# Three-layer graph network: FP32 rows and FP32 adjacency blocks in place of split BF16 ones, and 14 dense tiles in layer 1 in place of 10

## The reference, cut to what matters

```python
# x: 6250 x 256 FP32 nodes, 100000 edges sorted by dst, and a self loop on each node
deg  = segment_sum(1, dst);  dinv = rsqrt(deg);  norm_edge = dinv[src] * dinv[dst]
h = x
for W, b in ((W1, b1), (W2, b2), (W3, b3)):     # 256->512, 512->512, 512->256
    m = h @ W
    h = relu(segment_sum(m[src] * norm_edge[:, None], dst) + b)
out = layernorm(x + h)
```

## Time and profile before

| what | before |
|---|---|
| median of three runs (2494.5 to 2496.02) | 2496.0 us |
| the profiled execution's own time | 2488.2 us |
| its span, first to last instruction | 2486.4 us |
| PE busy / PEld busy | 2271.8 us (91%) / 1562.8 us (63%) |
| POOL busy | 1753.4 us (71%) |
| DVE / ACT busy | 1027.0 us (41%) / 521.7 us (21%) |
| mean granted clock of TensorE | 0.965 of full speed |
| moved by DMA | 568.24 MB, 229 GB/s |

### The profile page before, as it was taken

How to read it: one execution, slowest core, us unless ns; L and a number is a source line. 1 busy time by engine, 2 the same in 40 slices (tenths; PEclk the granted TensorE clock), 3 DMA queues, 4 the chain that set the end, 5 groups by cost and what they waited for, 6 DMA issues and landing times.

```text
span 2486.4 us, 42327 instructions
## 1 busy us (share of the span) xinstructions
PE 2271.8 (91%) x13351; PEld 1562.8 (63%) x13352; DVE 1027.0 (41%) x1307; ACT 521.7 (21%) x1322; POOL 1753.4 (71%) x1837
## 2 busy tenths in 40 slices
PE   6977799898999998999999999999988799999998
PEld 6855577676777773444444444444444688888887
DVE  8877333233333313444444444444422233333332
ACT  6611223222222312222222222222211000000000
POOL 5177777777777756777777777777776776767674
PEclk9788999999999999999999999999999899999999
DMA  6335666666666656888888888888887888888784
GB/s 215 119 118 184 222 203 206 201 198 205 192 209 190 208 170 204 253 272 268 267 264 264 263 267 264 264 268 258 275 260 236 261 257 249 252 248 255 245 247 140
DMA packets 231550, 568.24 MB, mean 229 GB/s; under 512 B 39868, under 2 KB 95795, under 8 KB 231475
## 3 DMA queue, kind: packets, MB, share of 16 engines
q0 software_dynamic: 126752, 399.62, 54.6%
q1 hardware_dynamic: 88371, 126.81, 14.5%
q10 hardware_dynamic: 16352, 40.77, 4.9%
HBM read 476.69 MB, written 90.36 MB: 228 GB/s over the span
## 4 chain that ended last, share of the span: by engine, by line
PE 55%; POOL 16%; issue 13%; DMA 7%; POOLq 4%; DVE 3%; ACT 0%; ACTq 0%; DVEq 0%; SPq 0%
POOL rows L671 16%; PE ps_acc L1511 9%; PE ps_h L1600 8%; PE ps_T L1600 7%; PE ps_o L1567 6%; DMA rows<-table,idx 5%; PE ps_d L1612 5%; PE ps_acc L1515 5%; PE ps_d L1515 4%; PE ps_h L1555 3%; PE ps_d L1511 3%; POOLq L680 3%; PE ps_d L1469 2%; DMA rows<-table_parts,idx 1%; PE ps_e L1588 1%
## 5 line engine op out<-in xcount | busy, mean ns | idle before, releaser
L671 POOL DMA_INDIRECT rows<-table,idx x912 | 870.0, 954 | 300.9 <-issue 264.7
L671 POOL DMA_INDIRECT rows<-table_parts,idx x884 | 837.1, 947 | 324.0 <-issue 268.2
L892 DVE SCALAR_TENSOR_TENSOR sel<-ps_e,firsts,dstT 128x1152 f32<-128x1152 f32 (+1 forms) x222 | 314.7, 1418 | 684.9 <-PE ps_acc L1511 253.9
L1515 PE MATMUL ps_acc<-rows,sel 128*128 128x512 f32 (+2 forms) x1122 | 489.8, 568 | 82.8 <-DMA rows<-table,idx 55.5
L1515 PE MATMUL ps_d<-rows,sel 128*128 128x512 f32 (+1 forms) x850 | 413.3, 616 | 41.3 <-DMA rows<-table,idx 41.2
L1511 PE MATMUL ps_acc<-rows,sel 128*128 128x256 bf16 (+1 forms) x2196 | 360.1, 280 | 50.5 <-DMA rows<-table_parts,idx 21.7
L1515 PEld LDWEIGHTS ps_acc<-rows,sel 128*128 128x128 f32 x1122 | 209.2, 202 | 250.0 <-issue 149.3
L1511 PEld LDWEIGHTS ps_acc<-rows,sel 128*128 128x128 bf16 x2196 | 217.9, 100 | 93.9 <-issue 37.8
L1515 PEld LDWEIGHTS ps_d<-rows,sel 128*128 128x128 f32 x850 | 152.8, 195 | 196.4 <-issue 119.2
L1567 PE MATMUL ps_o<-w,hT 128*128 128x512 f32 (+1 forms) x784 | 269.2, 486 | 1.2 <-ACT hT L1272 1.2
L1612 PE MATMUL ps_d<-parts,made_tiles 128*128 128x256 bf16 x1470 | 229.2, 272 | 0.5 <-issue 0.4
(11 more groups left out here) (190 smaller groups left out, 1902.8 us busy)
## 6 DMA issues: line engine op xcount, KB each, us to landing
built<-made_tiles SPq DMA_DIRECT2D x72, 384.0 KB
made_tiles<-built ACTq DMA_DIRECT2D x72, 384.0 KB
rows<-table,idx POOLq DMA_INDIRECT x912
rows<-table_parts,idx POOLq DMA_INDIRECT x884
table<-made SPq DMA_DIRECT2D x49, 256.0 KB
acc<-table SPq DMA_DIRECT2D x49, 256.0 KB
built<-made_tiles SPq DMA_DIRECT2D x24, 416.0 KB
made_tiles<-built ACTq DMA_DIRECT2D x24, 416.0 KB
```

The source lines that it names most:

```text
L671: pool.indirect_dma_start(out=to, out_offset=None, in_=its[0:nodes, :], in_offset=bass.IndirectOffsetOnAxis(ap=idx[:, of, k:k + 1], axis=0 ...
L892: v.scalar_tensor_tensor(to[:, k:k + FRONT, :], numbers.unsqueeze(1).broadcast_to([P, FRONT, P]), firsts[:, bass.ds(t, 1)], dstT[:, bass.d ...
L1515: return mm(to[:, 0:w], sel[:, k, :], rows_of[phase][:, k, 0:w] if first is None else first, start=start, stop=stop)
```

## The change

The BF16 parts are gone from all of it: `parts`, `table_parts`, `split_x`, `split`, the stores of parts and the waits for them. `whole` (128 x 49 x 256 FP32) takes the place of `parts`; layer 1 holds x scaled there, and layer 2's ACT writes its result straight into it, without waiting for `made_free`. Every gathered slot of layers 1 and 3 is one FP32 product of 256 columns.

A dense step is one FP32 product too, and its block must be FP32: a single buffer `wide` (128 x 49 x 128). ACT fills it from the BF16 block, piece by piece (`widen`, four copies of 1664 or 1536 columns for a tile), each as soon as PE has used that piece of the dense tile before (`dense_piece`). PE waits for each piece (`widened`). In layer 3, ACT loads the block after next once a piece is widened.

In layer 1, 14 tiles are dense and 35 gathered: seven plain windows, then 14 macros of two windows each. The loop of two macros runs six times. Layer 2 builds 10 blocks in place of 14, in its first 30 windows.

```diff
-DENSE_1 = 10
+DENSE_1 = 14
-PARTS = 3
-    PER = 3
+    PER = 2
-        parts = sb("parts", [P, T, PARTS, C], BF16)
-        xs = parts[:, :, :, :].rearrange("p t i c -> p (t i c)")[:, 0:2 * T * C].bitcast(F32).rearrange(
-            "p (t c) -> p t c", c=C)
+        whole = sb("whole", [P, T, C])
+        xs = whole
+        wide = sb("wide", [P, T, P])
...
-                        if phase == 2:
-                            pool.wait_ge(parts_stored, 16 * (T - 1))
...
-            def split_x(units):
...
-            def split(t):
...
+            def widen(q, of, pieces):
+
+                for piece in pieces:
+                    lo_h, hi_h = PIECES[piece]
+                    act.wait_ge(dense_piece, len(PIECES) * q + piece + 1)
+                    act.sem_inc(act_step, 1)
+                    nc.scalar.activation(wide[:, lo_h:hi_h, :], making[of][:, lo_h:hi_h, :], ACT.Copy).then_inc(widened, 1)
+
+            def widen_built(m, of, pieces):
+                act.wait_ge(self_added, m + 1)
+                widen(m, of, pieces)
...
@@ ACT, first window of a macro
                             scale_dense(m - 1)
+                            widen(m, 1 - of, range(len(PIECES) - 1, len(PIECES)))
+                            if half is not None:
+                                keep_pairs(*half, range(0, PAIRS // 2))
                             keep_aggT(s, aggT[:, 0:C], 0)
+                            if half is not None:
+                                keep_pairs(*half, range(PAIRS // 2, PAIRS))
                             relus(s)
...
+                    if build:
+                        widen_built(m + 1, of, range(len(PIECES) - 1))
...
-                if in_parts:
-                    row = rows_parts[:, k, :] if first is None else first
-                    for i in range(PARTS):
-                        ins = mm(to[:, 0:C], sel_parts[:, k, :], row[:, i * C:(i + 1) * C], start=start and i == 0,
-                                 stop=stop and i == PARTS - 1)
-                    return ins
...
-                    for i in range(PARTS):
-                        ins = mm(ps_dense_1, making[of][:, h, :], parts[:, h, i, :], start=(h == 0 and i == 0),
-                                 stop=(h == T - 1 and i == PARTS - 1))
+                    wait_widened(k, h)
+                    ins = mm(ps_dense_1, wide[:, h, :], whole[:, h, :], start=(h == 0), stop=(h == T - 1))
...
-                DENSE_CUTS = [0, 11, 29, T]
+                DENSE_CUTS = [0, 16, T]
```

More of the change, by code:

```diff
@@ L389, in gnn_program @@
         y_d_stored = sem("y_d_stored")
-        X_UNITS = [(47 - 2 * i, 2, False) for i in range(22)] + [(3, 2, True), (1, 2, True), (0, 1, True)]
-        X_DONE = [0, 0, 2, 5, 9, 15, 21, len(X_UNITS)]
-        assert T == 49 and ASIDE == 5 and len(X_DONE) <= MACRO
+        assert MACRO > 6
         block = ctx.enter_context(nc.Block())
@@ L492, in store @@
                         w = WIDTH[phase + 1]
-                        sp.dma_start(table[phase + 1][bass.ds(t * P, P), :], made[:, 0:w]).then_inc(stored, 16)
+                        its = made[:, 0:w]
+                        if phase == 1 and per == 1:
+                            its = whole[:, bass.ds(t, 1), :].rearrange("p a c -> p (a c)")
+                        sp.dma_start(table[phase + 1][bass.ds(t * P, P), :], its).then_inc(stored, 16)
                         sp.wait_ge(stored, 16 * s + 16)
@@ L1111, in macro @@
                         steady(0, MACRO + PER * m + b, (MACRO + PER * odd + b) % 2, hots,
-                               (m, place_of(m, True), of) if b == 0 else None, last=not build and b == PER - 1, in_parts=True)
+                               (m, place_of(m, True), of) if b == 0 else None, last=not build and b == PER - 1)
                 macro(0, 0, 0)
@@ L1119, in one_window, with six @@
                 to_next(0)
-                def six(i, first=False):
+                def six(i):
                     for b in range(6):
@@ L1128, in six @@
                                (q, place_of(q, False), u) if part == 2 else None)
-                        if not first or b > 0:
-                            split(t - 2)
-                six(0, True)
-                with v_.Fori(1, SIXES) as i:
+                with v_.Fori(0, SIXES) as i:
                     six(i)
@@ L1282, in relus, with make @@
                     relu_T(ps_h[:, m * P:(m + 1) * P], b1T, m)
[L1284 removed]
+            def make(phase, t, s, per=1):
                 w = WIDTH[phase + 1]
                 act.wait_ge(o_done, s + 1)
[L1287 removed]
+                if phase == 1 and per == 1:
+                    to = whole[:, bass.ds(t, 1), :].rearrange("p a c -> p (a c)")
+                else:
+                    to = made[:, 0:w]
+                    act.wait_ge(made_free, s + 1)
                 act.sem_inc(act_step, 1)
[L1289 removed]
+                nc.scalar.activation(to, ps_o[:, 0:w], ACT.Copy, scale=dinv[:, bass.ds(t, 1)]).then_inc(made_ready, 1)
             def tile(phase, t, n, s, per, built_half=None):
@@ L1516, in add_slot, with slots @@
                           start=start, stop=stop)
-            def slots(phase, n, ks, first, need=None, beside=None, ps=None, in_parts=False):
+            def slots(phase, n, ks, first, need=None, beside=None, ps=None):
                 to = ps_acc if ps is None else ps
@@ L1590, in build, with wait_widened @@
                 ins.then_inc(pair_built, 1)
+            def wait_widened(q, h):
+                for piece, (lo_h, _) in enumerate(PIECES):
+                    if h == lo_h:
+                        pe.wait_ge(widened, len(PIECES) * q + piece + 1)
             def dense(i, into, hs):
```

260 lines of the change are left out of this document (86 added, 174 removed).

## The result

| | before | after |
|---|---|---|
| median of the runs | 2495.25 us (four runs, 2490.92 to 2496.02) | 2799.02 us (four runs, 2796.4 to 2802.53) |
| profiled execution, span | 2488.2 us, 2486.4 us | 2799.73 us, 2798.0 us |

The changed kernel is slower: the ratio is 1.1222, with a 95% interval of 1.1203 to 1.1242. The forecast was 2800 us, and slower with a chance of 0.97.

What follows compares the result with a forecast made beforehand. PE was taken to bound layers 1 and 3, POOL layer 2. 147.2 - 5.4 + 163.2 = +305.0 on the profiled 2488.2 us gives 2793.2; for a median 2801, rounded to 2800 us, range 2765 to 2840.

Steps and rivals of the forecast that it cites:

- Prices: On PE, a step or slot goes from 0.327 us (three BF16 products) to 0.430 us (one FP32 product), plus 0.103 us.
- Layer 3: PE-bound windows go from 21.7 to 28.5 us, 24 of them, with ACT's widening hidden: +163.2 us.
- Layer 2: POOL's 16 gathers a window stay and hide the removed `split` and four blocks: 0, lower end -10 us.
- Into layer 3: POOL's 5.39 us wait before layer 3's first gather goes, `stored` being next late: -5.4 us, other end 0.
- Layer 1, start: Six windows ahead of the first macro, which opens at 257.5 us instead of 300.17.
- Layer 1, macros: Twelve macros of 58.9 us, first 52.9, last 54.2; layer 1 ends at 1071.4 us instead of 924.22, +147.2 us.
- The new wait: In a layer 1 macro's first window PE waits for ACT's copies behind the last piece's widening, losing 2.0 us.
- The loop's gap: Layer 1's smaller loop body leaves no idle PE at the turn back, 15.4 us before; other end +26 us.
- (a): Rival: the gap where layer 1's loop turns back stays, 2826 us; chance 0.12.
- (b): Rival: ACT too late in layer 1, a widening costing 2.5 us: +39 us, 2839 us; 0.14 with other late waits.
- (c): Rival: not slower, as an FP32 product of 256 columns costs little; at 0.22 us some 2350 us; chance 0.02.
- (d): Rival: POOL's relief outweighs PE's cost in layer 1, which shrinks 80 us; total near 2570 us; 0.05, or part of it.

Runs made afterwards that it cites:

- the BF16 product: Changed kernel with each dense step of layer 3 as one BF16 product from the upper halves of the FP32 words: 3047.25 us, ratio 0.9878 to before.
- the widening behind the relus: Changed kernel with ACT widening the last piece after the relus instead of before the building copies in a macro's first window: 2780.92 us, ratio 1.1165 to before.
- the FP32 variant: Changed kernel with PE's layer 1 loop holding four macros, three passes, instead of two macros, six passes: 3169.39 us, ratio 1.0272 to before, on a slower chip.

## Why the prediction was right

**Prices.** The whole forecast hung on 0.430 us for an FP32 product against 0.327 us for three BF16 ones. Timeline of PE in layer 3 of after, alternating slots and dense steps:

```profile
2280.02 0.59 PE L1440 MATMUL ps_d<-rows,sel 128*128 128x256 f32 x2
2280.45 1.46 PE L1525 MATMUL ps_T<-whole,wide 128*128 128x256 f32 x6
2281.74 0.59 PE L1440 MATMUL ps_d<-rows,sel 128*128 128x256 f32 x2
2282.18 1.46 PE L1525 MATMUL ps_T<-whole,wide 128*128 128x256 f32 x6
```

Start to start: 0.43 us for the slot's product, 1.29 and 1.30 for three steps. The price holds when two sources of weights alternate. The FP32 weight loads take twice as long as the BF16 ones, 190 ns against 98 for L1600 before, and stay under the products:

```profile
L1525 PEld LDWEIGHTS ps_T<-whole,wide 128*128 128x128 f32 x1176 | 223.9, 190 | 30.6
```

**Layer 3: right, and for the stated reason.** 28.49 us a window against 28.5 forecast, PE at 100.00 of 100. The doubled widening shows the cover to be there, and the BF16 product shows PE's price to be the cause.

**Layer 2: right.** 20.08 us a window after, 20.02 before. The 2.6 us in 48 windows have no cause that I know; the traces of the other three FP32 kernels on the first kind of chip have 958.90, 961.32 and 962.88 us for them, so that the difference lies within their spread. Four blocks fewer and no `split` gave nothing, since POOL sets the pace (75.81 of 100); with the 14 blocks of the kernel with ten dense tiles the layer is no longer either.

**Into layer 3: the wait fell as forecast, and the gain was given back.** POOL's wait did fall, from the 5.39 us of the earlier trace rows, and the next late thing was `stored`, as named:

```profile
2072.48 0.95 POOL L627 DMA_INDIRECT rows<-table,idx  x1 [1.84 <-DMA table<-whole]
```

That is 3.6 of the 5.4 us. They were then given back. By the first sum of layer 3 the gain is 0.2 us. The DMA's part of the profile for the 25 us in which layer 3's first window gathers (1930 to 1955 before, 2076 to 2101 after), packets, MB, share of 16 engines; before first:

```profile
q0 software_dynamic: 1280, 3.93, 47.0%
q10 hardware_dynamic: 1152, 3.21, 35.2%
```

```profile
q10 hardware_dynamic: 1498, 4.21, 47.4%
q0 software_dynamic: 867, 2.36, 28.1%
...
rows<-table,idx POOLq DMA_INDIRECT x20, 5.7
```

ACT loads two whole blocks when layer 3 begins, as before, and since it widens the first pieces at once it now follows with a third one, piece by piece, from 2092.96 us on. These loads share the DMA engines with the gathers of a window in which PE has nothing but gathered slots. A gather takes 5.7 us to land there, against 3.5 for the whole program. PE's last wait for rows in that window ends 27.9 us after POOL's first gather (2072.48 to 2100.38), before it was 23.8 (1927.07 to 1950.85). I had listed the loads of the block after next as part of the change and had not asked what they run into. No run was made to move them, so that this is read from the trace and not shown by an experiment. And it is not the same each time: the stretch took 26.99 us before and 26.82 after, but 23.82 with ten dense tiles, 25.83 with the widening behind the relus and 24.99 with every widening written twice. In the first two of these POOL does not wait at all there. So FP32 gained between 0.2 and 3.2 us here, and the 5.4 of the forecast in no trace.

**Layer 1, start: right within 2.3 us.** The first macro opens at 255.17 us, forecast 257.5, before 300.17. The terms given for the forecast add up to 256.9 and not to 257.5.

**Layer 1, macros: right in the sum, with small errors that cancel.** From 311.54 to 1016.61 us, twelve macros, 58.76 us each, forecast 58.9. The new wait is 1.6 us (20.5 in 13), not 2.0; PE's own work and what lies between windows are 0.3 us more than forecast. The widening costs 1480 ns for 1536 columns, 1.5 forecast. The first macro took 56.4 us against 52.9, with a granted clock of 0.94 in its first window, and the last one 54.2 as forecast. The three widenings in the second window do fit: they end at 717.64 + 4.32 = 721.96, and ACT is next needed at 723.27.

```profile
717.64 4.32 ACT L1235 ACTIVATE wide<-made_tiles 128x1664 f32<-128x1664 bf16 x3
```

**The loop's gap: right that it goes, and that the body's size decides it.** Idle PE put down to issue fell from 15.4 us to nearly nothing, and the instruction queue from 51 to 25 packets:

```profile
PE ps_acc L1440 <- issue: 1.3, 2, 0.9
```

I argued from the body's size, and the runs bear it out from both sides. The BF16 loop with fourteen dense tiles has before's number format and back edges but 718 matmul records in place of 872: it is not refetched and does not stop. The FP32 loop of four macros has 1144: it is refetched. What I had from the earlier trace rows alone is the cost. The longer body stopped PE for 1.5 to 2.0 us at a back edge, and before's for 4.5 to 5.5. What makes before's stop so long is open, as the two were not traced on the same chip.

**The sum.** 2793.2 us were forecast for the profiled execution, and it took 2799.73. Of the 6.5 us between, 5.2 are the gain into layer 3 that was given back and 2.6 are layer 2, against 1.2 in the other direction in the small terms. For the median I had added 7.8 us to the profiled time, for the difference to the three runs of before; after's profiled execution is at its median, which hid the miss. The match at 2800 is better than the working behind it by those 6 us.

**The rivals.** (a) Not seen, there is no gap. (b) The widening takes 1.48 us and not 2.5; at twice its cost the loss of 80 us would have come. (c) holds only for a cheap product, and was tried in layer 3 alone. (d) fell: POOL's share dropped to 52.96 in layer 1 and nothing was won by it. The runs with ten FP32 tiles and fourteen BF16 ones show that the more tiles are dense, the slower it gets, in FP32 by some 80 us and in BF16 by at most 51.

## What to carry to other kernels

Price a change of data type by start-to-start times of the very shapes in the trace, and multiply by the number of products only where PE is the bound: here layers 1 and 3 gave 310 of 312 us. Moving work from an engine that is not the bound (POOL's gathers in layer 1) to the one that is (PE's dense steps) is a loss however much it relieves the first. A wait that ends earlier is a gain only if what it releases finds its own path free; look for what else will be queued on the DMA engines at that moment, above all what the same change put there.

## What the runs showed of the hardware

**A record count says little.** Layer 3 went from 916 records in 100 us to 465, at a granted clock of 1.00 (2.4 GHz) in both and with PE full in both.

**A loop's body is kept up to a size, and beyond it a back edge costs.** While PE's loop with 718 matmul records in its body (and as many weight loads) ran, one instruction packet was moved from 430 to 880 us, and PE did not stop at the back edges. With 872 it was 24 packets in the same stretch, and a stop of 4.5 to 5.5 us at each of three back edges, on the same kind of chip and both in BF16. Written out, that code moved as many packets in all (53 against 51) and was 0.6 to 0.8% faster in three comparisons.

**A wait of 6 us costs more than 6 us on PE.** Behind one such wait, in the kernel with every widening written twice, the granted clock was 0.53 for the 3.9 us looked at, and over twelve macros the same products kept PE busy 1.8 us longer in each.

**Chips differ, and a full engine hardly feels it.** On the slower chips before took 3084.6 to 3090.6 us in place of 2493. The median durations of single instructions and the PE-bound windows of layer 3 are the same there (28.47 us against 28.49). Many of the hand-overs from one engine to the other are longer there. PE idles more, and its granted clock is lower: before with its loop written out had 0.897 on average, before on the first kind of chip 0.965, and the same 13351 records kept PE busy for 2445.4 us in place of 2271.8. By engine, the chain of work that ended last, in the loop of four macros on such a chip and in after on the first one:

```profile
PE 60%; another core or an unknown queue 18%; issue 10%; POOL 4%; ACT 3%; DVE 2%; DMA 1%; POOLq 1%; ACTq 1%; DVEq 0%
```

```profile
PE 68%; POOL 11%; issue 10%; DMA 6%; POOLq 3%; DVE 1%; ACT 1%; ACTq 0%; DVEq 0%; SPq 0%
```

A window of layer 2 took 23.9 us there in place of 20.1, with POOL busy for 63 of 100 in place of 75. What delays the hand-overs, and what the "unknown queue" is, stays open. It bears on how a change is judged: on such a chip the FP32 variant was only 2.7% slower than before, on the first one after was 12.2% slower. Layer 3 shows why. Where PE is full, in the FP32 variant, its 24 windows took 692.9 us there against 683.8; where POOL is just behind, in before with its loop written out, 660.6 us against 520.6.
